# Linear attention: all four banks of masked scores through ScalarE's copy and GpSimd's select, none through VectorE

## The chip, the cores and the metric

One Trainium2 chip, one of its cores. The metric is the time of one execution on the device in microseconds (us), and the median of several runs is compared.

## The reference, cut to what matters

Two transformer layers over x of 8 x 1024 x 256 in float32: a half-weighted feed-forward block, attention, and another feed-forward block in each. The change lies in the attention of the first layer, which is linear attention with 16 heads of 16 columns, worked off in chunks, with a causal mask inside a chunk and a running state S between chunks:

```python
def step(S, chunk):
    q_c, k_c, v_c = chunk
    inter = jnp.einsum('bhde,bthe->bthd', S, q_c)
    scores = jnp.einsum('bthd,bshd->bhts', q_c, k_c)
    scores = jnp.where(causal, scores, 0.0)
    intra = jnp.einsum('bhts,bshd->bthd', scores, v_c)
    S = S + jnp.einsum('bthd,bthe->bhde', v_c, k_c)
    return (S, inter + intra)
```

The second layer's attention is softmax attention with 16 heads over all 1024 positions, causal. The feed-forward blocks of the second layer have a small router and low-rank experts.

## The kernel before, in words

The kernel works on the batch rows one after another. For each of the eight rows there are two "fronts" (c = 0 and c = 1, 512 tokens each), which compute the first layer and the beginning of the second, and two "tails" with the rest of the second layer. Beside them runs the "core", the softmax attention of an earlier row, cut into 768 steps: at each step TensorE computes score tiles (`tscore`, L798), ScalarE turns them into exponentials (`core_act`, L1343), TensorE multiplies these by the values (`values`, L817) at every other step, and a further product (`score`, L783) feeds the row maxima that VectorE takes (L1137, L1140). GpSimd makes the diagonal blocks of the exponentials causal (L1497).

The order is written out by hand. Every stage is a generator for each engine. `weave` runs a common count of ticks: in a tick it issues the core's first part, then the next piece of front 0, the core's second part, the piece of front 1, and so on. `STEPS` says how many core steps (0, 1 or 2) a tick has, and a batch row takes 120 ticks with 96 steps. An engine takes its instructions strictly in the order in which `weave` issued them, so an instruction that waits holds everything issued behind it.

The fronts and tails of all rows share three PSUM banks in turn (`f_take`, `f_filled`, `f_freed`, `f_gone`): the n-th taker may start when the taker of n - 3 has been read out of its bank.

The linear attention of one front (`lin_pe`, `lin_dve`, `lin_act`, `lin_pool`) handles four blocks j of 128 tokens, in three ticks each, here called the first, second and third tick of j. Its scores for 16 heads fill four banks sc0 to sc3:

- first tick: TensorE computes the output of block j - 1 (L648, L655) and then, in `scores(j, 0)`, the banks sc0 and sc1 (L620, eight matmuls);
- second tick: after the core's `tscore`, TensorE computes in `scores(j, 1)` the banks sc2 and sc3 (L620 again), and then `state` (L631). It takes both banks before its first matmul. VectorE masks sc0 and sc1 in `masked` (L944), from PSUM to the SBUF tile `scm`. ScalarE copies out the output of j - 1 (L1249);
- third tick: ScalarE, after the exponentials of that tick's core step and after the piece of front 0 if the block is front 1's, copies sc2 and sc3 to `scm` in `raw` (L1245), and GpSimd zeroes their upper half in place in `select` (L1409). Then `state` on VectorE (L956) and on GpSimd (L1422).

Which bank `scores(j, 1)` has to wait for depends on what other takers lie between. With none, sc2 takes the bank of the block output of j - 1 and sc3 that of sc0. Where another stage's matmul takes a bank between sc1 and sc2 (this is so in blocks 1 and 2 of front 0, and 0 and 1 of front 1), sc2 needs the bank of sc0 and sc3 that of sc1.

Of the kernel before, what the change touches and what calls it, by code (L numbers as in the profile page):

```python
# [12 lines left out]
ALU = mybir.AluOpType  # L13
# [3 lines left out]
P = 128  # L17
# [7 lines left out]
NC = T // CH  # L25
G = 4
# [31 lines left out]
def macaron(nc, a, out):  # L58
    ctx = ExitStack()
    with ctx:  # L60
        def sb(name, shape, dt=F32):
            return ctx.enter_context(nc.sbuf_tensor(name, shape, dt))

        def sem(name):
            return ctx.enter_context(nc.semaphore(name))
# [15 lines left out]
        mask01 = sb("mask01", [P, P])  # L81
# [32 lines left out]
        def ar(at, *shape):  # L114
            n = math.prod(shape)
            at = int(at * KB)
            v = arena[:, at:at + n]
            names = "abcd"[:len(shape)]
            return v.rearrange(f"p ({' '.join(names)}) -> p {' '.join(names)}", **dict(zip(names[1:], shape[1:]))) if len(shape) > 1 else v
# [10 lines left out]
        scm = ar(27, G, CH)  # L130
# [36 lines left out]
        def ps(i, n=1):  # L167
            return bank[i // 2][:, (i % 2) * CH:(i % 2) * CH + n * CH]
# [210 lines left out]
        s = {n: sem(n) for n in plain_names}  # L379
# [76 lines left out]
        if True:  # L456

            with nc.Block() as block:
# [10 lines left out]
                def f_bank(*key):  # L469
                    return ps(5 + ftab[key] % 3)  # L470

                def f_filled(eng, *key):
                    eng.wait_ge(s["f_full"], ftab[key] + 1)

                def f_freed(*key):
                    return f_free[ftab[key] % 3]

                def f_gone(eng, *key):
                    eng.wait_ge(f_free[ftab[key] % 3], ftab[key] // 3 + 1)
# [107 lines left out]
                def lin_pe(c, b):  # L587
# [47 lines left out]
                    def outputs(j):  # L635
                        t = 4 * c + j
                        if t == 1:
                            f_gone(nc.tensor, 0, b, "st", 0)
                        elif t:
                            nc.tensor.wait_ge(s["st"], 6 * b + t - 1)  # L640
                        nc.tensor.wait_ge(s["vs"][c], 4 * b + j + 1)
                        for i in range(2):
                            f_gone(nc.tensor, c, b, "sc", j, i)
                        nc.tensor.wait_ge(s["sel"][c], 8 * b + 2 * j + 2)
                        bk = f_take(c, b, "y", j)
                        if t:
                            for k in range(KT):
                                mm(bk[:, k * P:(k + 1) * P], ssb[:, (t - 1) % 2, k], qT[:, k, j * P:(j + 1) * P], start=k == 0,  # L648
                                   stop=False, skip_group_check=True)
                        vrow = vlin[:, j].rearrange("p q d -> p (q d)")  # L650
                        for k in range(KT):
                            for o in range(2):
                                for r in range(G):
                                    at = 3 * DK * (4 * k + r) + DK * o
                                    last = mm(bk[HP * r:HP * (r + 1), k * P:(k + 1) * P], vrow[:, at:at + HP],  # L655
                                              scm[:, r, (2 * k + o) * P:(2 * k + o + 1) * P], start=t == 0 and k == 0 and o == 0,
                                              stop=o == 1, skip_group_check=True, tile_position=(0, HP * r))
                        last.then_inc(s["f_full"], 1)
# [208 lines left out]
                def updated(q, b, n):  # L867
                    nc.vector.wait_ge(s["xu"][q], 4 * b + n)
# [53 lines left out]
                def lin_dve(c, b):  # L922
                    yield from ln_dve(c, b, 1, xns, lambda: updated(c, b, 2))
                    yield from idle(4)
                    for j in range(4):
                        nc.vector.wait_ge(s["ksq"][c], 4 * b + j + 1)
                        nc.vector.reduce_sum(kvar[:, j], ksq[:, j % 2].rearrange("p (h d) -> p h d", h=H), AX).then_inc(s["kvar"][c], 1)
                        yield
                    nc.vector.wait_ge(s["kvar"][c], 4 * b + 4)
                    kvf, krf, ktf = (v[:].rearrange("p t h -> p (t h)") for v in (kvar, krs, ktmp))  # L930
                    nc.vector.tensor_scalar(kvf, kvf, EPS, None, ALU.add).then_inc(s["newton"][c], 1)
                    nc.vector.wait_ge(s["newton"][c], NEWTON * b + 1)
                    rsqrt(krf, kvf, ktf, s["newton"][c], NEWTON * b + 1)
                    yield

                    def masked(j):
                        if c == 0 and j == 0 and b >= 3:
                            for o in range(NC):
                                nc.vector.wait_ge(s["xout"][o], 16 * (b - 2))
                        elif c == 0 and j == 0 and b:  # L940
                            nc.vector.wait_ge(s["qkout"][1], 64 * b)
                        for i in range(2):
                            f_filled(nc.vector, c, b, "sc", j, i)
                            nc.vector.tensor_tensor(scm[:, i].rearrange("p (j c) -> p j c", j=G),  # L944
                                                    f_bank(c, b, "sc", j, i).rearrange("p (j c) -> p j c", j=G),
                                                    mask01[:].unsqueeze(1).broadcast_to([P, G, P]), ALU.mult).then_inc(
                                                        f_freed(c, b, "sc", j, i), 1)

                    def state(j):
                        t = 4 * c + j  # L950
                        if t == NT - 1:
                            return
                        f_filled(nc.vector, c, b, "st", j)
                        if t >= 2:
                            nc.vector.wait_ge(s["st"], 6 * b + t - 1)
                        nc.vector.tensor_tensor(smask if t else ssb[:, 0],  # L956
                                                f_bank(c, b, "st", j)[:, 0:D].rearrange("p (k c) -> p k c", k=KT),
                                                bdmask[:].rearrange("p h d -> p (h d)").unsqueeze(1).broadcast_to([P, KT, P]),
                                                ALU.mult).then_inc(f_freed(c, b, "st", j), 1)

                    def added(p):
                        f_filled(nc.vector, c, b, "lo", p)
                        xs = xq(c)[:, 2 * p:2 * p + 2]
                        nc.vector.tensor_tensor(xs, xs, f_bank(c, b, "lo", p).rearrange("p (t c) -> p t c", t=2), ALU.add).then_inc(
                            f_freed(c, b, "lo", p), 1)

                    for j in range(4):
                        if j == 3:
                            added(0)
                        yield  # L970
                        masked(j)
                        yield
                        state(j)
                        yield
                    yield from idle(3)
                    added(1)
                    yield
# [231 lines left out]
                def lin_act(c, b):  # L1209
# [27 lines left out]
                    def raw(j):  # L1237
                        if c == 0 and j == 0 and b >= 3:
                            for o in range(NC):
                                nc.scalar.wait_ge(s["xout"][o], 16 * (b - 2))  # L1240
                        elif c == 0 and j == 0 and b:
                            nc.scalar.wait_ge(s["qkout"][1], 64 * b)
                        for i in (2, 3):
                            f_filled(nc.scalar, c, b, "sc", j, i)
                            nc.scalar.copy(scm[:, i], f_bank(c, b, "sc", j, i)).then_inc(f_freed(c, b, "sc", j, i), 1)  # L1245

# [132 lines left out]
                def lin_pool(c, b):  # L1379
# [23 lines left out]
                                                ALU.mult).then_inc(s["vs"][c], 1)  # L1403

                    def select(j):
                        for i in (2, 3):
                            f_gone(nc.gpsimd, c, b, "sc", j, i)
                            v = scm[:, i].rearrange("p (j c) -> p j c", j=G)
                            nc.gpsimd.affine_select(out=v, in_=v, compare_op=ALU.is_ge, fill=0.0, base=0, pattern=[[0, G], [1, P]],  # L1409
                                                    channel_multiplier=-1).then_inc(s["sel"][c], 1)  # L1410
# [236 lines left out]
```

## Time and profile before

| | |
|---|---|
| median of 3 runs | 2860.79 us (2854.37 to 2863.7) |
| the profiled execution | 2854.86 us, of which the span from the first to the last instruction 2853.1 us |
| mean granted TensorE clock | 0.946 of full speed |
| busy share of the span | TensorE 91%, VectorE 65%, ScalarE 43%, GpSimd 26% |
| chain of work that ended last | TensorE 71%, VectorE 16%, ScalarE 2%, GpSimd 1%, DMA 1% |

The busy share is a mean over stages with different limits; the chain follows back from the last instruction to what released each step. Batch rows 2 to 7 of the linear attention repeat nearly the same pattern, about 331 us apart; the rows of the trace are taken from batch row 4 (front 0 at 1300 to 1344 us, front 1 at 1370 to 1416 us).

### The profile page before, as it was taken

To read this page: it belongs to the slowest core of one execution; us is meant where nothing else is said; L and a number is where in the kernel's file an instruction comes from. 1 tells how busy PE (TensorE), PEld (TensorE's weight loads), DVE (VectorE), ACT (ScalarE), POOL (GpSimd) and SP (SyncE) were. 2 spreads that over 40 slices of the span, in tenths; PEclk is the share of its full clock that TensorE was granted. 3 is DMA by queue.
4 is the path that set the end of the run, shared out by engine and by line. 5 is a ranking of instruction groups with operands and counts; after the bars stand their busy time and mean duration, and the time that the engine had idled before them with its cause. 6 is when DMAs were issued, how large, how long until landed. Compare 5 with 4: busy or idle time off the path is not lost.

```text
span 2853.1 us, 45542 instructions
## 1 busy us (share of the span) xinstructions
PE 2595.9 (91%) x15278; PEld 1723.8 (60%) x15278; DVE 1841.9 (65%) x5524; ACT 1228.5 (43%) x2805; POOL 747.9 (26%) x1285
## 2 busy tenths in 40 slices
PE   5875899989999999999999999999999999998996
PEld 4663566556656666566655666566665666655644
DVE  4454666776667667676676766776667766776642
ACT  2321244454444444444444444454444444444452
POOL 2421222223222232223322232222222233221111
PEclk8996899999999999999999999999999999999998
DMA  2024013411334112422145113332134221343311
GB/s 61 1 68 119 18 24 75 128 39 30 72 88 108 41 43 64 130 64 58 24 110 131 37 32 72 94 102 54 29 79 124 55 58 36 103 112 74 80 31 48
DMA packets 135248, 193.93 MB, mean 68 GB/s; under 512 B 46239, under 2 KB 108014, under 8 KB 124654
## 3 DMA queue, kind: packets, MB, share of 16 engines
q1 hardware_dynamic: 133440, 190.89, 26.4%
q8 instruction: 129, 2.11, 0.3%
q14 instruction: 97, 0.79, 0.1%
q10 hardware_dynamic: 1582, 0.13, 0.0%
HBM read 122.29 MB, written 67.63 MB: 67 GB/s over the span
## 4 chain that ended last, share of the span: by engine, by line
PE 71%; DVE 16%; issue 2%; ACT 2%; POOL 1%; DMA 1%; SPq 0%; DVEq 0%; ACTq 0%; POOLq 0%
PE bank L798 10%; PE bank L817 9%; PE bank L783 9%; PE bank L620 4%; PE bank L711 4%; DVE bank L1137 4%; PE bank L551 4%; PE bank L569 4%; PE bank L600 3%; PE bank L560 3%; PE bank L725 3%; PE bank L530 3%; PE bank L712 2%; PE bank L655 2%; PE bank L768 2%
## 5 line engine op out<-in xcount | busy, mean ns | idle before, releaser
L1343 ACT ACTIVATE pexp<-bank 128x512 f32<-128x512 f32 (+3 forms) x1536 | 677.3, 499 | 575.4 <-PE bank L798 575.2
L1137 DVE CUSTOM_DVE_ANT_0 bank<-bank,maskneg 128x256 f32<-128x256 f32 (+3 forms) x1024 | 484.1, 511 | 263.0 <-PE bank L783 258.9
L798 PE MATMUL bank<-stq,stk 128*128 128x512 f32 (+3 forms) x1536 | 547.5, 427 | 30.9 <-ACT pexp L1343 24.1
L783 PE MATMUL bank<-stk,stq 128*128 128x512 f32 (+3 forms) x1536 | 506.4, 394 | 62.5 <-DVE mxa L1137 24.6
L798 PEld LDWEIGHTS bank<-stq,stk 128*128 128x128 f32 x1536 | 267.9, 195 | 320.1 <-ACT pexp L1343 190.5
L1140 DVE TENSOR_REDUCE mxa<-bank 128x1 f32<-128x512 f32 x512 | 345.8, 683 | 146.5 <-PE bank L783 142.3
L1497 POOL TENSOR_SCALAR_AFFINE_SELECT pexp<-pexp 128x256 f32<-128x256 f32 x512 | 212.4, 422 | 763.6 <-ACT pexp L1343 763.4
L783 PEld LDWEIGHTS bank<-stk,stq 128*128 128x128 f32 x1536 | 281.5, 198 | 174.4 <-issue 136.0
L817 PE MATMUL bank<-pexp,vsm 128*32 128x512 f32 (+3 forms) x3072 | 343.8, 521 | 20.1 <-POOL pexp L1497 19.9
L1409 POOL TENSOR_SCALAR_AFFINE_SELECT arena<-arena 128x512 f32<-128x512 f32 x128 | 78.2, 634 | 393.4 <-ACT arena L1245 393.3
L530 PE MATMUL bank<-ident,arena 128*128 128x128 f32 x768 | 117.9, 301 | 46.7 <-DVE arena L861 42.6
L620 PE MATMUL bank<-arena 32*128 32x256 f32 x1024 | 152.3, 416 | 8.6 <-DVE arena L944 5.6
L944 DVE TENSOR_TENSOR arena<-bank,mask 128x512 f32<-128x512 f32 x128 | 82.3, 684 | 92.6 <-PE bank L620 92.6
L530 PEld LDWEIGHTS bank<-ident,arena 128*128 128x128 f32 x768 | 101.5, 157 | 64.9 <-DVE arena L861 46.6
L551 PE MATMUL bank<-arena,wk 128*128 128x256 f32 x512 | 133.1, 410 | 4.7 <-DVE arena L885 4.5
L817 PEld LDWEIGHTS bank<-pexp,vsm 128*32 128x32 f32 x3072 | 62.7, 110 | 123.3 <-issue 94.7
L1162 ACT COPY xnT<-bank 128x512 f32<-128x512 f32 x160 | 88.6, 601 | 96.6 <-PE bank L530 96.0
L1360 POOL TENSOR_SCALAR varep<-mv 128x4 f32<-128x4 f32 x96 | 22.5, 234 | 408.6 <-DVE mv L855 408.2
L620 PEld LDWEIGHTS bank<-arena 32*128 32x128 f32 x1024 | 92.1, 193 | 56.3 <-issue 37.9
L861 DVE TENSOR_SCALAR arena<-x,mv,rstd 128x256 f32<-128x256 f32 x320 | 117.9, 429 | 11.4 <-POOL rstd L1362 10.7
L560 PE MATMUL bank<-wr,arena 128*128 128x256 f32 x512 | 122.9, 383 | 0.1
L551 PEld LDWEIGHTS bank<-arena,wk 128*128 128x128 f32 x512 | 104.7, 208 | 27.6 <-issue 6.1
(186 smaller groups left out, 4051.6 us busy)
## 6 DMA issues: line engine op xcount, KB each, us to landing
stq<-q_halves SPq DMA_DIRECT2D x128, 256.0 KB
arena<-rope_table SPq DMA_DIRECT2D x16, 1024.0 KB
q_halves<-arena SPq DMA_DIRECT2D x32, 512.0 KB, 2.8
k_halves<-arena SPq DMA_DIRECT2D x32, 512.0 KB, 2.9
stk<-k_halves SPq DMA_DIRECT2D x64, 256.0 KB
stk<-k_halves SPq DMA_DIRECT2D x128, 128.0 KB
v_rows<-arena SPq DMA_DIRECT2D x16, 544.0 KB, 4.1
vsm<-v_rows SPq DMA_DIRECT2D x16, 544.0 KB, 3.8
```

What stands on the lines that cost most here:

```text
L530: last = nc.tensor.transpose(bk[:, t * P:(t + 1) * P], src[:, t, k * P:(k + 1) * P], ident[:])
L551: last = mm(bk[:, m * D:(m + 1) * D], wk0[:, k, m * P:(m + 1) * P], xmA[:, h, k], start=k == 0, stop=k == KT - 1)
L560: last = mm(bk[:, i * D:(i + 1) * D], xmB[:, p, k, i * P:(i + 1) * P], wr0[:, k], start=k == 0, stop=k == KT - 1)
L620: last = mm(bks[i][:, k * D:(k + 1) * D], khT[rows, k, j * P:(j + 1) * P], qbd[rows, j % 2, k], start=k == 0, stop=k == KT - 1, skip_group ...
L783: last = mm(bk[:, col:col + n], stq[b_][:, h % 2, qb * P:(qb + 1) * P], stk[b_][:, h % 2, k0:k0 + n], start=True, stop=True)
L798: mm(ps(j)[:, 0:n], stk[b_][:, j, kb * P:(kb + 1) * P], stq[b_][:, j, (c + 1) * CH - n:(c + 1) * CH], start=True, stop=True).then_inc(s["t ...
L817: last = mm(ps(2)[HP * j:HP * (j + 1), CH - n:CH], vsm[:, kb, at:at + HP], pexp[:, (u - 1 + j // 2) % NPX, j % 2, 0:n], start=kb == 0, sto ...
L861: nc.vector.tensor_scalar(dst[:, t], xs[:, t], mv[:, q, t, 0:1], rstd[:, q, t:t + 1], ALU.subtract, ALU.mult).then_inc(s["xn"][q], 1)
L1137: last = nc.vector.tensor_tensor_reduce(out=sc, in0=sc, in1=maskneg[:, CH - n:CH], scale=1.0, scalar=LOWEST, op0=ALU.add, op1=ALU.max, acc ...
L1140: last = nc.vector.reduce_max(dst, sc, AX)
L1343: nc.scalar.activation(pexp[:, u % NPX, j, 0:n], ps(j)[:, 0:n], ACT.Exp, scale=DK ** -0.5).then_inc(s["exp_done"], 1)
L1497: nc.gpsimd.affine_select(out=v, in_=v, compare_op=ALU.is_ge, fill=0.0, base=0, pattern=[[0, 2], [1, P]], channel_multiplier=-1).then_inc( ...
```

## The change

`masked` on VectorE goes, with its 128 tensor_tensor instructions. ScalarE's `raw` copies all four banks in the third tick, and GpSimd's `select` works on all four. The count of GpSimd's selects for which TensorE's output waits doubles accordingly.

```diff
                         for i in range(2):
                             f_gone(nc.tensor, c, b, "sc", j, i)
-                        nc.tensor.wait_ge(s["sel"][c], 8 * b + 2 * j + 2)
+                        nc.tensor.wait_ge(s["sel"][c], 16 * b + 4 * j + 4)
...
-                    def masked(j):
-                        if c == 0 and j == 0 and b >= 3:
-                            for o in range(NC):
-                                nc.vector.wait_ge(s["xout"][o], 16 * (b - 2))
-                        elif c == 0 and j == 0 and b:
-                            nc.vector.wait_ge(s["qkout"][1], 64 * b)
-                        for i in range(2):
-                            f_filled(nc.vector, c, b, "sc", j, i)
-                            nc.vector.tensor_tensor(scm[:, i].rearrange("p (j c) -> p j c", j=G),
-                                                    f_bank(c, b, "sc", j, i).rearrange("p (j c) -> p j c", j=G),
-                                                    mask01[:].unsqueeze(1).broadcast_to([P, G, P]), ALU.mult).then_inc(
-                                                        f_freed(c, b, "sc", j, i), 1)
-
...
-                        masked(j)
...
-                        for i in (2, 3):
+                        for i in range(0, 4):
                             f_filled(nc.scalar, c, b, "sc", j, i)
                             nc.scalar.copy(scm[:, i], f_bank(c, b, "sc", j, i)).then_inc(f_freed(c, b, "sc", j, i), 1)
...
                     def select(j):
-                        for i in (2, 3):
+                        for i in range(0, 4):
                             f_gone(nc.gpsimd, c, b, "sc", j, i)
```

## Rows read from the trace of the kernel before

**Rows 1.** The page's first part: busy time, share of the span, instructions.
```profile
PE 2595.9 (91%) x15278; PEld 1723.8 (60%) x15278; DVE 1841.9 (65%) x5524; ACT 1228.5 (43%) x2805; POOL 747.9 (26%) x1285
```

**Rows 2.** Windows of both fronts' linear attention: busy us (instructions), PEclk, DMA, GB/s.
```profile
1300.00:1344.00 44.00, 44.00 (x380) 32.14 (x380) 28.48 (x75) 20.15 (x46) 14.78 (x30) 1.00 0.22 52
1370.00:1416.00 46.00, 45.73 (x331) 31.45 (x331) 28.12 (x67) 18.21 (x37) 14.08 (x24) 0.93 0.13 27
```

**Rows 3.** Groups by line: mask, copy and select.
```profile
L1409 POOL TENSOR_SCALAR_AFFINE_SELECT arena<-arena 128x512 f32<-128x512 f32 x128 | 78.2, 634 | 393.4 <-ACT arena L1245 393.3
L944 DVE TENSOR_TENSOR arena<-bank,mask 128x512 f32<-128x512 f32 x128 | 82.3, 684 | 92.6 <-PE bank L620 92.6
L1245 ACT COPY arena<-bank 128x512 f32<-128x512 f32 x128 | 68.8, 589 | 87.0 <-PE bank L620 87.0
```

**Rows 4.** Timeline, front 0, block 1: start, us, instruction.
```profile
1312.32 1.13 PE L620 MATMUL bank<-arena 32*128 32x256 f32 x8
...
1316.76 1.13 PE L620 MATMUL bank<-arena 32*128 32x256 f32 x8
...
1316.90 0.66 ACT L1343 ACTIVATE pexp<-bank 128x256 f32<-128x256 f32 x2
...
1317.93 1.07 ACT L1245 COPY arena<-bank 128x512 f32<-128x512 f32 x2 [0.37 <-PE bank L620]
...
1318.58 1.22 POOL L1409 TENSOR_SCALAR_AFFINE_SELECT arena<-arena 128x512 f32<-128x512 f32 x2 [5.45 <-ACT arena L1245]
```

**Rows 5.** Timeline, front 0, blocks 0, 2 and 3: last ScalarE work, second half.
```profile
1303.01 1.09 ACT L1343 ACTIVATE pexp<-bank 128x512 f32<-128x512 f32 x2 [1.37 <-PE bank L798]
...
1305.08 1.13 PE L620 MATMUL bank<-arena 32*128 32x256 f32 x8
...
1329.43 1.13 PE L620 MATMUL bank<-arena 32*128 32x256 f32 x8
...
1329.48 0.45 ACT L1343 ACTIVATE pexp<-bank 128x128 f32<-128x128 f32 x2 [2.94 <-PE bank L798]
...
1337.67 1.09 ACT L1343 ACTIVATE pexp<-bank 128x512 f32<-128x512 f32 x2 [1.15 <-PE bank L798]
...
1338.03 1.13 PE L620 MATMUL bank<-arena 32*128 32x256 f32 x8
```

**Rows 6.** Timeline, front 1, blocks 0, 2 and 3: the same, and a mask.
```profile
1378.46 0.60 ACT L1183 ACTIVATE arena<-bank 128x512 f32<-128x512 f32 x1 [2.48 <-PE bank L551]
1378.59 0.73 PEld L620 LDWEIGHTS bank<-arena 32*128 32x128 f32 x8 [0.35 <-issue]
...
1402.66 1.08 ACT L1343 ACTIVATE pexp<-bank 128x512 f32<-128x512 f32 x2 [1.15 <-PE bank L798]
...
1404.38 0.73 PEld L620 LDWEIGHTS bank<-arena 32*128 32x128 f32 x8 [0.24 <-issue]
...
1411.31 1.29 DVE L944 TENSOR_TENSOR arena<-bank,mask 128x512 f32<-128x512 f32 x2 [0.29 <-PE bank L620]
1411.75 0.87 ACT L1343 ACTIVATE pexp<-bank 128x384 f32<-128x384 f32 x2 [1.09 <-PE bank L798]
...
1412.75 0.73 PEld L620 LDWEIGHTS bank<-arena 32*128 32x128 f32 x8 [0.84 <-DVE arena L944]
```

**Rows 7.** Windows over two idle gaps of TensorE and what follows each.
```profile
1511.30:1513.10 1.80, 0.02 (x1) 0.06 (x1) 1.76 (x9) 0.74 (x2) 0.65 (x2) 1.00 0.82 291
...
1514.20:1517.60 3.40, 3.40 (x16) 2.68 (x13) 2.80 (x10) 0.90 (x3) 0.67 (x2) 0.50 0.01 2
...
1553.00:1554.20 1.20, 0.04 (x1) 0.00 (x0) 1.20 (x9) 0.12 (x1) 0.70 (x2) 1.00 1.12 353
1554.20:1557.00 2.80, 2.77 (x23) 1.96 (x24) 2.02 (x9) 1.64 (x4) 1.22 (x3) 1.00 0.67 213
```

**Rows 8.** Windows of the same work in batch rows 4 and 5.
```profile
1302.25:1374.07 71.82, 69.94 (x496) 45.93 (x494) 47.62 (x131) 33.34 (x81) 24.51 (x44) 0.98 0.14 34
1636.22:1706.52 70.30, 68.42 (x495) 45.42 (x494) 46.10 (x129) 33.34 (x81) 24.52 (x44) 1.00 0.15 35
```

## The prediction

> **What bounds the kernel now.** I read the page first: TensorE is busy for 2595.9 of 2853.1 us, VectorE for 1841.9, ScalarE for 1228.5, GpSimd for 747.9 [rows 1]. That alone says that work taken from VectorE need not show and that work given to ScalarE need not hurt. What counts is the stretch in which the change lies, so I read the windows of the linear attention next. Front 0 takes 44 us there and TensorE is busy for all 44.00; front 1 takes 46 us and it is busy for 45.73, while VectorE works for 28.48 and 28.12, and ScalarE for 20.15 and 18.21 [rows 2]. In these stretches TensorE is the bound, and the chain of work that ended last runs through TensorE from block to block. So the question is one of order: does TensorE ever have to wait for a read-out that VectorE used to do early and ScalarE now does late? For that I read the groups of the three operations [rows 3] and then, block by block, the timeline [rows 4 to 6].
>
> **What the change removes and adds.** Removed from VectorE: 128 masks of 684 ns, 82.3 us busy in the trace [rows 3]. They lie beside a TensorE that is never idle, so I price the removal at nothing. Added to ScalarE: 128 copies of 589 ns, 75 us; added to GpSimd: 128 selects of 634 ns, 81 us [rows 3]. Both engines wait most of that time anyway: in block 1 of front 0 ScalarE waited 0.37 us for sc2 before its copies, and GpSimd 5.45 us before its selects [rows 4]. The first two selects of a block can run while TensorE fills sc2 and sc3, and the last select still ends about one select after the last copy. So the output's wait for GpSimd is late only by what TensorE itself is late. These instructions cost nothing as work.
>
> **What the change moves.** The reading of sc0 and sc1 moves from the second tick on VectorE to the third tick on ScalarE, behind that tick's exponentials. But `scores(j, 1)`, in TensorE's second tick, needs the bank of sc0 and in four of eight blocks that of sc1 too. Behind its wait in TensorE's queue stand sc2 and sc3, `state`, the core's values and scores and the next `tscore`, for which ScalarE, VectorE and GpSimd wait in turn. There is no deadlock in that: the exponentials ahead of ScalarE's copies need only the `tscore` issued just before.
>
> The new stall of a block is the time at which ScalarE has emptied the needed bank, less the time at which TensorE started the second half before. Three constants come from rows: two copies take 1.07 us together [rows 4] at 0.59 each [rows 3], so the second starts 0.48 after the first; an instruction that waits for nothing starts the same 0.11 before the reported end of the one ahead (0.59 less 0.48). So after the end of ScalarE's previous instruction sc0 is free at +0.48 and sc1 at +0.96. And TensorE starts 0.15 after the release: masks until 1412.60, matmuls from 1412.75 [rows 6]. A stall is therefore the ScalarE end + 0.63 (sc0 needed) or + 1.11 (sc1 needed), less the old start.
>
> Front 0:
> - Block 0 (sc0): its third tick has no core step. ScalarE is free at 1304.10, + 0.63 = 1304.73, before the old start at 1305.08 [rows 5]: 0.
> - Block 1 (sc1): 1317.56 + 1.11 - 1316.76 = 1.91 us [rows 4].
> - Block 2 (sc1): 1329.93 + 1.11 - 1329.43 = 1.61 us [rows 5].
> - Block 3 (sc0): 1338.76 + 0.63 - 1338.03 = 1.36 us [rows 5].
>
> Front 1:
> - Block 0 (sc1): 1379.06 + 1.11 - 1378.59 = 1.58 us; block 1 repeats the same pattern, with the receptance's tanh in place of the relu: 1.58 us [rows 6].
> - Block 2 (sc0): 1403.74 + 0.63 = 1404.37, just in time for 1404.38 [rows 6]: 0.
> - Block 3 (sc0): 1412.62 + 0.63 - 1412.75 = 0.50 us [rows 6]. Here TensorE had waited for the mask already, and that wait is in the old start.
>
> That is 8.54 us for a batch row. Since TensorE has no slack in these stretches, it is late by this afterwards, and the chain is with it. `state` needs sc1's bank where sc3 needs only sc0's; sc1 is out 0.48 us after sc0 while the second half takes 1.13 us [rows 5], so no second wait follows. Batch rows 2 to 7 have this pattern: 6 x 8.54 = 51 us. For rows 0 and 1, with no or little core work and so with ScalarE sooner at hand, I bound each by nothing and 8.5 us and take 10 us for both. Direct stalls: 61 us (51 to 68).
>
> **The clock.** Five stalls of a batch row last 1.36 to 1.91 us, in a TensorE that had none there. What an idle gap does is seen elsewhere: after a gap of 1.8 us at 1511 us the granted clock was 0.50 (1.2 in place of 2.4 GHz) for 3.4 us, after one of 1.2 us at 1553 us it stayed at 1.00 [rows 7]. The new stalls lie between these two, nearer to the longer one. The price of a fall is bounded above by 3.4 x 0.5 = 1.7 us, where TensorE would have been busy throughout. The same work took 71.82 us in batch row 4 at a mean clock of 0.98 and 70.30 in row 5 at 1.00 [rows 8]: 1.5 us. I take 1.5, and three of the five stalls with a fall (bounds none and five): 4.5 us a row, 27 for six rows, 3 for the first two: 30 us (0 to 60).
>
> The Trainium skill, "TensorE: Matmul & The Clock Gate" (HAM oscillation), warns of waits for data longer than any stall worked out here; if only those count, no fall comes and the sum stays at 61 us. Rows 7 speak against it, since a gap of 1.8 us was followed by a lower clock.
>
> The last row of rows 6 also shows TensorE's queue at such a wait: 0.84 us idle for the mask, with nothing taken ahead. The same page (Architectural detail) says that weight loads can be pulled ahead of matmuls in flight; eight such loads take 0.73 us in rows 6, 0.09 each, and if one were ahead at each of five stalls in six rows, the stalls would come to 58 in place of 61 us.
>
> **The sum.** 61 + 30 = 91 us. Against the profiled execution (2854.9 us: its span of 2853.1 and 1.8 around it) that is 2946 us. The runs' median lies 5.9 us above that execution, so I forecast 2952 us, 3.2% slower.
>
> **Rivals.**
> - Stalls without falls of the clock: 2861 + 61 = 2922 us. For it: the stalls are shorter than the gap that brought a fall in rows 7. Chance 0.22.
> - Half of the delay is won back later, because VectorE, ScalarE and the transfers run ahead while TensorE stands, and TensorE's later waits for them shrink: 2861 + 30 = 2891 us. For it: outside these stretches TensorE is not always busy (91% over the span). Against: most of these waits follow a serial chain that starts from TensorE's own result and is shifted with it. Chance 0.10.
> - Every one of the five stalls brings a fall, or falls that last longer, and the first two batch rows stall fully: 68 + 60 = 128 and more, 2989 us and up. Chance 0.08.
> - Faster: VectorE sets the pace (it has 16% of the chain that ended last), and the 82.3 us taken from it come off the end: at most 2861 - 82 = 2779 us. It decides if TensorE's waits for the masks and for the maxima queued behind them are worth more than 8.5 us a batch row. Against: one wait for a mask of 0.84 us stands in rows 6, and rows 2 leave 0.27 us of idle time in 90. Chance 0.05.
> - No change: TensorE's wait is hidden after all, because ScalarE reaches its copies before TensorE the second half in nearly all blocks, as in blocks 0 and 2 of the two fronts. 2861 us. It would need ScalarE 1.4 to 1.9 us earlier. Chance 0.05.
> - My forecast, with one to four falls in a batch row: 0.50. Its own range is 2932 to 2972 us.
>
> **Range and chances.** From the rival without falls, a little widened towards the one that wins some back, up to all five falls: 2900 to 2990 us. A measurement of this kernel can tell about 0.3% from no change, 8.6 us. Slower 0.90, same 0.05, faster 0.05.
>
> **What the next profile would show.** If right: TensorE's L620 waits for ScalarE's L1245 in blocks 1, 2, 3 of front 0 and 0, 1, 3 of front 1, by 1.3 to 2 us (0.5 in the last), about 50 us in all; block 0 of front 0 and block 2 of front 1 without a wait. TensorE's busy share in the two windows falls from all to about nine tenths, the distance between batch rows grows from 331 to 340 us or more, and new stretches at clock 0.50 stand behind the stalls. L1245 and L1409 count 256 each at unchanged durations. The prediction is wrong if L620 does not wait, if the distance of the batch rows grows by much less than the stalls' sum (then it is won back), or if TensorE's later waits for VectorE shrink by as much.

## The result, and the profile after

The changed kernel takes 2945.23 us (median of 4 runs, 2925.3 to 2951.69) against 2857.58 us (4 runs); the ratio is 1.0294, 95% interval 1.0268 to 1.0320. It is slower by some 85 us. The forecast was 2952 us, 3.2% slower. The profiled execution took 2942.78 us, its span is 2941.0 us.

The first part of the page of the changed kernel, which answers to [rows 1], and from its fifth part the groups that answer to [rows 3] (lines below 944 have moved up by 13 or 14, so the copy is L1231, the select L1395, the exponentials L1329):

```profile
PE 2618.4 (89%) x15278; PEld 1751.6 (60%) x15278; DVE 1769.8 (60%) x5396; ACT 1292.4 (44%) x2933; POOL 833.7 (28%) x1413
...
L1395 POOL TENSOR_SCALAR_AFFINE_SELECT arena<-arena 128x512 f32<-128x512 f32 x256 | 160.8, 653 | 382.6 <-ACT arena L1231 382.6
L620 PE MATMUL bank<-arena 32*128 32x256 f32 x1024 | 151.6, 413 | 66.0 <-ACT arena L1231 63.0
L1231 ACT COPY arena<-bank 128x512 f32<-128x512 f32 x256 | 137.8, 595 | 84.1 <-PE bank L620 84.1
```

VectorE gave up 72 us of busy time, ScalarE and GpSimd took over 64 and 86, and none of this is the loss (the first experiment keeps all of it and loses nothing). The loss is in TensorE's row: before `scores` (L620) it now sits idle for 66.0 us, 63.0 of it until ScalarE's copy; in the kernel before it was 8.6 us. TensorE's idle time over the span rose from 257.2 (2853.1 less 2595.9 [rows 1]) to 322.6 us (2941.0 less 2618.4), by 65.4 us. Its busy time rose by 22.5 us, though it does the same 15278 matmuls: some of them ran at the lower clock. The two make the 87.9 us by which the span grew.

The windows of the linear attention in batch row 4, which answer to [rows 2]:

```profile
1337.00:1382.00 45.00, 40.33 (x309) 29.27 (x308) 21.96 (x60) 19.42 (x44) 17.38 (x31) 0.96 0.17 38
1414.00:1460.00 46.00, 42.56 (x325) 30.35 (x318) 21.58 (x56) 20.64 (x41) 17.02 (x29) 0.96 0.13 27
```

A TensorE that was busy for 44.00 of 44 us is now busy for 40.33 of 45. The timeline of front 0, block 1 shows why ([rows 4] before), and under it stand the second halves of front 0, blocks 2 and 3, and of front 1, blocks 0, 1 and 3 ([rows 5, 6] before):

```profile
1352.63 0.59 PE L798 MATMUL bank<-stq,stk 128*128 128x256 f32 x2
...
1353.51 0.66 ACT L1329 ACTIVATE pexp<-bank 128x256 f32<-128x256 f32 x2
1354.04 1.09 ACT L1231 COPY arena<-bank 128x512 f32<-128x512 f32 x2
...
1355.25 0.76 PEld L620 LDWEIGHTS bank<-arena 32*128 32x128 f32 x8 [2.12 <-ACT arena L1231]
1355.28 1.13 PE L620 MATMUL bank<-arena 32*128 32x256 f32 x8 [1.84 <-ACT arena L1231]
...
1371.11 1.13 PE L620 MATMUL bank<-arena 32*128 32x256 f32 x8 [1.54 <-ACT arena L1231]
...
1381.07 1.13 PE L620 MATMUL bank<-arena 32*128 32x256 f32 x8 [1.28 <-ACT arena L1231]
...
1419.95 1.13 PE L620 MATMUL bank<-arena 32*128 32x256 f32 x8 [1.51 <-ACT arena L1231]
...
1436.08 1.13 PE L620 MATMUL bank<-arena 32*128 32x256 f32 x8 [1.51 <-ACT arena L1231]
...
1457.81 1.13 PE L620 MATMUL bank<-arena 32*128 32x256 f32 x8 [0.42 <-ACT arena L1231]
```

TensorE computes the score tiles of the core, then wants the banks of sc0 and sc1. ScalarE first makes the exponentials of just these tiles (1353.51 to 1354.17), then copies sc0 and sc1 (until 1355.13), and TensorE goes on 0.15 us later.

### The profile page after: what moved, and what is told of

Read it like the earlier page. It is cut to its first block, busy times and chain, and to the rows that moved or that the text cites. A ratio compares the mean times of both kernels' runs of the same rounds, so it can differ in the third digit from the quotient of the medians.

```text
span 2941.0 us, 45663 instructions
## 1 busy us (share of the span) xinstructions
PE 2618.4 (89%) x15278; PEld 1751.6 (60%) x15278; DVE 1769.8 (60%) x5396; ACT 1292.4 (44%) x2933; POOL 833.7 (28%) x1413
## 4 chain that ended last, share of the span: by engine, by line
PE 69%; DVE 14%; ACT 4%; issue 3%; DMA 2%; POOL 1%; SPq 1%; DVEq 0%; ACTq 0%; POOLq 0%
PE bank L798 9%; PE bank L783 8%; PE bank L817 8%; PE bank L620 4%; PE bank L711 4%; PE bank L551 4%; DVE bank L1123 3%; PE bank L569 3%; PE bank L560 3%; PE bank L600 3%; PE bank L725 3%; PE bank L530 3%; PE bank L712 2%; PE bank L655 2%; PE bank L768 2%
## 5 line engine op out<-in xcount | busy, mean ns | idle before, releaser
L1329 ACT ACTIVATE pexp<-bank 128x512 f32<-128x512 f32 (+3 forms) x1536 | 677.1, 498 | 573.9 <-PE bank L798 573.5
L817 PE MATMUL bank<-pexp,vsm 128*32 128x512 f32 (+3 forms) x3072 | 336.7, 511 | 20.2 <-POOL pexp L1483 20.0
L1395 POOL TENSOR_SCALAR_AFFINE_SELECT arena<-arena 128x512 f32<-128x512 f32 x256 | 160.8, 653 | 382.6 <-ACT arena L1231 382.6
L620 PE MATMUL bank<-arena 32*128 32x256 f32 x1024 | 151.6, 413 | 66.0 <-ACT arena L1231 63.0
L1231 ACT COPY arena<-bank 128x512 f32<-128x512 f32 x256 | 137.8, 595 | 84.1 <-PE bank L620 84.1
L620 PEld LDWEIGHTS bank<-arena 32*128 32x128 f32 x1024 | 94.7, 190 | 112.1 <-ACT arena L1231 66.5
L1346 POOL TENSOR_SCALAR varep<-mv 128x4 f32<-128x4 f32 x96 | 22.6, 235 | 409.8 <-DVE mv L855 409.4
L560 PE MATMUL bank<-wr,arena 128*128 128x256 f32 x512 | 130.1, 400 | 0.1
```

The source lines that it names most:

```text
L560: last = mm(bk[:, i * D:(i + 1) * D], xmB[:, p, k, i * P:(i + 1) * P], wr0[:, k], start=k == 0, stop=k == KT - 1)
L620: last = mm(bks[i][:, k * D:(k + 1) * D], khT[rows, k, j * P:(j + 1) * P], qbd[rows, j % 2, k], start=k == 0, stop=k == KT - 1, skip_group ...
L817: last = mm(ps(2)[HP * j:HP * (j + 1), CH - n:CH], vsm[:, kb, at:at + HP], pexp[:, (u - 1 + j // 2) % NPX, j % 2, 0:n], start=kb == 0, sto ...
L1329: nc.scalar.activation(pexp[:, u % NPX, j, 0:n], ps(j)[:, 0:n], ACT.Exp, scale=DK ** -0.5).then_inc(s["exp_done"], 1)
```

## The experiments

All ratios are against the kernel before on the same chip. In the diffs the comments behind # are added here, and where a run changes how many banks ScalarE and GpSimd take, the counts that TensorE waits for change with it. After each expectation stands what was measured; the profiled executions of all of them are put together behind the last one.

**ScalarE early.** The changed kernel, with the copies of sc0 and sc1 one tick earlier on the same engine.

```diff
-                    def raw(j):
+                    def raw(j, part):
...
-                        for i in range(0, 4):
+                        for i in (2 * part, 2 * part + 1):
...
                         if j:
                             heads_out(j - 1)
+                        raw(j, 0)
                         yield
-                        raw(j)
+                        raw(j, 1)
```

> The changed kernel, but ScalarE copies sc0 and sc1 in the second tick (right after the output of j - 1) and sc2 and sc3 in the third. The work on every engine is that of the changed kernel. If the loss is the order (ScalarE reads sc0 and sc1 only after the third tick's exponentials), it is gone: sc0 and sc1 are free before TensorE wants their banks, and the time is that of the kernel before, 2850 to 2868 us. If the loss is the added work of ScalarE (64 us more busy) and GpSimd (86 us more busy), it stays: 2935 to 2955 us.

Measured: 2859.9 us (10 runs) against 2856.25, ratio 1.0003, interval 0.9986 to 1.0020. The whole loss is gone, with every operation of the change still in place. The group of TensorE's `scores` and that of the copies in this run:

```profile
L620 PE MATMUL bank<-arena 32*128 32x256 f32 x1024 | 152.1, 416 | 6.0 <-ACT arena L1231 3.0 <-POOL arena L1381 2.2 <-ACT arena L1220 0.9
L1231 ACT COPY arena<-bank 128x512 f32<-128x512 f32 x256 | 137.6, 590 | 112.2 <-PE bank L620 112.2
```

The same 256 copies, but it is now ScalarE that waits for TensorE. Its timeline in front 0, block 1:

```profile
1308.85 1.13 PE L620 MATMUL bank<-arena 32*128 32x256 f32 x8
...
1310.01 1.07 ACT L1231 COPY arena<-bank 128x512 f32<-128x512 f32 x2 [0.56 <-PE bank L620]
...
1313.29 1.13 PE L620 MATMUL bank<-arena 32*128 32x256 f32 x8
```

ScalarE empties sc0 and sc1 by 1311.08, and TensorE needs them at 1313.29.

**VectorE late.** The kernel before, with the masks one tick later on VectorE.

```diff
-                        masked(j)
                         yield
+                        masked(j)
                         state(j)
```

> The kernel before, but VectorE's masks moved to the third tick, ahead of its state. No engine gets any work that it had not. If lateness alone costs, TensorE's second half waits for VectorE, which first takes the maxima of the tick before: in block 1 of front 0 its masks would end at about 1318.8 where the second half started at 1316.76, a stall of about 2.2 us, and now in block 0 too. 2940 to 3020 us. If the added work on ScalarE and GpSimd is the cause, nothing changes: 2850 to 2870 us.

Measured: 3062.68 us (4 runs), ratio 1.0724, interval 1.0682 to 1.0766. No engine has more to do than in the kernel before, and it is the slowest of all. The theory of the order holds in kind, but the time is a miss: it lies 43 us above the upper end of my range. Front 0, block 1:

```profile
1408.88 0.70 DVE L1137 CUSTOM_DVE_ANT_0 bank<-bank,maskneg 128x512 f32<-128x512 f32 x1 [4.59 <-PE bank L783]
...
1409.49 1.28 DVE L944 TENSOR_TENSOR arena<-bank,mask 128x512 f32<-128x512 f32 x2
1410.89 1.30 PEld L620 LDWEIGHTS bank<-arena 32*128 32x128 f32 x8 [2.38 <-DVE arena L944]
1410.92 2.00 PE L620 MATMUL bank<-arena 32*128 32x256 f32 x8 [2.08 <-DVE arena L944]
```

And a window of this run that begins just behind that stall:

```profile
1411.00:1417.80 6.80, 6.80 (x24) 5.18 (x24) 1.30 (x5) 1.07 (x2) 3.35 (x6) 0.50 0.00 0
```

The stall of 2.08 us is the one foretold (2.2). The matmuls behind it took 2.00 us for what takes 1.13 elsewhere [rows 4], with the granted clock at 0.50.

**GpSimd's half.** The kernel before, with VectorE copying in place of masking, and GpSimd selecting all four banks.

```diff
-                            nc.vector.tensor_tensor(scm[:, i]..., f_bank(c, b, "sc", j, i)..., mask01..., ALU.mult)
+                            nc.vector.tensor_copy(scm[:, i], f_bank(c, b, "sc", j, i))
...
-                        for i in (2, 3):      # select on GpSimd
+                        for i in range(4):
```

> The kernel before, but VectorE copies sc0 and sc1 unmasked, in the second tick as before, and GpSimd selects all four banks. That is GpSimd's part of the change alone: 128 more selects, and the output waits for them. By my theory it costs nothing, 2850 to 2868 us, since the first two selects run before the third copy ends. If the selects are what is late, 2 more of 0.63 us in each of 64 blocks, up to 80 us more: 2900 to 2940 us.

Measured: 2864.09 us (10 runs) against 2856.25, ratio 1.0023, interval 1.0007 to 1.0038. The 128 selects more cost some 7 us at the most (2 to 11 by the interval) of the 85. In the profile the idle time is the same as before (257.3 us for 257.2) and TensorE's busy time is 6 us longer at a clock of 0.944 for 0.946, so the few us lie in the clock; that the selects bring this about is not shown, since the run with ScalarE early has as many selects and a ratio of 1.0003. TensorE's wait for them before the output was 2.9 us in this run, in 9 waits, so it is no new wait: that of the changed kernel is 2.9 us in 9 too, and the kernel before had 3.1 in 9.

**One bank late.** Only sc0 goes to ScalarE's third tick; sc1 stays with VectorE's mask.

```diff
-                        for i in range(2):    # masked on VectorE
+                        for i in (1,):
...
-                        for i in (2, 3):      # raw on ScalarE, select on GpSimd
+                        for i in (0, 2, 3):
```

> Only sc0 moves to ScalarE's third tick, sc1 stays with VectorE's mask in the second. By the theory of the order the four stalls that ended with sc1 end with sc0, 0.48 us earlier, the others stay: 8.3 less 1.9 is 6.4 us a batch row, with some fewer falls of the clock: 2912 to 2935 us. If the loss went with the number of banks that ScalarE and GpSimd take over, half of it would stay: 2900 us. If only stalls long enough for a fall of the clock counted, most would be gone: below 2890 us.

Measured: 2952.09 us (4 runs), ratio 1.0323, interval 1.0282 to 1.0364: a miss, no faster than with both banks late. The stalls did shrink, the four that had ended with sc1, by 0.35 to 0.42 us each where I had worked out 0.48: TensorE's wait for ScalarE's copies is 50.1 us in place of 63.0. Its whole idle time is 22.6 us less than in the changed kernel, about 10 us more than these stalls account for. But its busy time is 27.9 us more, because the mean granted clock fell from 0.942 to 0.931. Windows over three stalls of this run, each followed by one of what came after, and the beginning of front 1:

```profile
1351.71:1353.17 1.46, 0.00 (x0) 0.00 (x1) 0.76 (x2) 1.20 (x4) 0.19 (x1) 1.00 0.00 0
1355.20:1358.60 3.40, 3.40 (x11) 2.46 (x10) 1.01 (x5) 0.21 (x1) 3.14 (x6) 0.50 0.00 0
1367.57:1368.71 1.14, 0.01 (x1) 0.00 (x1) 1.10 (x2) 0.92 (x3) 0.16 (x1) 1.00 0.04 14
1369.00:1373.00 4.00, 4.00 (x29) 2.88 (x27) 2.42 (x10) 2.16 (x4) 2.55 (x5) 1.00 1.05 229
1377.41:1378.66 1.25, 0.00 (x0) 0.00 (x1) 1.25 (x7) 1.14 (x3) 0.05 (x1) 1.00 0.00 0
1379.10:1385.90 6.80, 6.80 (x35) 5.43 (x32) 2.13 (x9) 3.18 (x7) 2.83 (x6) 0.50 0.28 82
...
1413.20:1423.40 10.20, 9.71 (x30) 5.53 (x29) 6.34 (x10) 2.13 (x5) 2.91 (x4) 0.50 0.00 0
```

A stall of 1.25 us was followed by 6.8 us at the lower clock with TensorE busy throughout, some 3.4 us of loss; and where front 1 begins, the clock stayed low for 10.2 us. That place is not without a fall in the kernel before either:

```profile
1370.80:1377.60 6.80, 6.80 (x25) 4.05 (x18) 5.45 (x9) 1.09 (x2) 1.52 (x2) 0.50 0.00 0
```

**The other bank late.** The same work moved, but sc1 in place of sc0.

```diff
-                        for i in (1,):        # masked on VectorE
+                        for i in (0,):
...
-                        for i in (0, 2, 3):   # raw on ScalarE, select on GpSimd
+                        for i in (1, 2, 3):
```

> As the run with one bank late, but the other bank: sc0 stays with VectorE's mask in the second tick, sc1 moves to ScalarE's third. The same work moves between the engines. By the theory of the order only the four blocks whose second half needs sc1 stall, by ScalarE's end + 0.63 less the old start: 1.43, 1.13, 1.10 and 1.10, and block 3 of front 0 by some 0.3 at its state: 5.1 us a batch row, 35 to 40 us, and 0 to 40 us from stretches of the lower clock, which the run with sc0 late showed to be larger than I had taken: 2895 to 2935 us. If work moved is what costs, it is the 2952 us of that run.

Measured: 2909.09 us (4 runs), ratio 1.0168, interval 1.0150 to 1.0185, within the range of the order and 43 us below the run with the other bank late. TensorE's idle time is 35 us above that of the kernel before, as worked out. So the time does not go with how much work has moved: the same work costs 50 us here and 96 there. Of the difference between the two profiled executions the order accounts for 8 us, the idle time; 30 us are TensorE's longer busy time, at a clock of 0.931 for 0.939.

**sc0 copied twice.** The changed kernel, with one more copy on ScalarE ahead of the release of sc0.

```diff
                             f_filled(nc.scalar, c, b, "sc", j, i)
+                            if i == 0:
+                                nc.scalar.copy(scm[:, 3], f_bank(c, b, "sc", j, i))
```

> The changed kernel with one copy more on ScalarE in each block, of sc0 and ahead of its release. Each stall becomes 0.48 us longer and block 2 of front 1 gets one of about 0.45: 7 x 0.48 is 3.4 us a batch row, 24 us over seven, and some more stretches of the lower clock, up to 10 us: 2965 to 2985 us. If ScalarE's copies cost only as work hidden beside TensorE, the 64 more of them (31 us busy) change nothing against the changed kernel: 2945 us.

Measured: 3004.52 us (4 runs), ratio 1.0493, interval 1.0463 to 1.0523. Slower, as the order says, but by 59 us more than the changed kernel where I expected 20 to 40. In its profile the idle time rose by 26 us, as worked out (24). The profiled execution is the slowest of the four (3025.49 us, clock 0.921; the others 0.927 to 0.931), and in it TensorE's busy time is 57 us longer than in the changed kernel; at the median that leaves about 33 us to the clock, where I had taken up to 10.

**Roles swapped.** ScalarE copies sc0 and sc1 in the second tick with GpSimd's select; VectorE masks sc2 and sc3 in the third.

```diff
-                        for i in range(2):    # masked on VectorE, now in the third tick
+                        for i in (2, 3):
...
-                        for i in (2, 3):      # raw on ScalarE, now in the second tick; select on GpSimd
+                        for i in range(2):
```

> ScalarE copies sc0 and sc1 in the second tick and GpSimd selects them; VectorE masks sc2 and sc3 in the third tick, which need no select behind them. By the theory of the order there is no stall at the second half; the end of a block is a mask (0.68 us) in place of a copy and a select. If VectorE is at hand in the third tick, the waits of the output for GpSimd (3 us in all before) go: 2840 to 2860 us. If VectorE comes late to sc2, the next taker of its bank waits: 2865 to 2900 us.

Measured: 2864.75 us (10 runs) against 2860.53, ratio 1.0015, interval 1.0003 to 1.0027. No gain: a tie with the kernel before, and the time lies between the two ranges. TensorE's wait for GpSimd before the output is gone, as expected, but the idle time over the span is 6 us more. No version here beats the kernel before.

**The changed kernel again.**

> The changed kernel unchanged, for the spread of its times and clocks. If the part of its loss beyond the stalls is lost to stretches of lower clock, the time of a run goes with its mean granted clock, and a run at the clock of the kernel before (0.946) takes its time plus the idle time added alone, 2855 + 65 = 2920 us, where 0.938 gives some 2950 us. If the clock were beside the point, runs at equal clock would differ as much as runs at different ones.

Measured: 2938.96 us (6 runs), ratio 1.0278, interval 1.0253 to 1.0303. The six runs with their mean clocks: 2925.49 (0.946), 2932.61 (0.944), 2937.96 (0.942), 2939.96 (0.942), 2950.33 (0.938), 2950.67 (0.939). Time times clock is 2767 to 2771 us in all six, while the times spread over 25 us: the spread is the clock's. The fastest run, at the clock of the kernel before, lies 5 us above the 2920 us expected.

The profiled executions side by side (idle is the span less TensorE's busy time; the last two columns are the differences from the kernel before, us):

| | span | TensorE busy | idle | clock | idle more | busy more |
|---|---|---|---|---|---|---|
| before | 2853.1 | 2595.9 | 257.2 | 0.946 | | |
| changed | 2941.0 | 2618.4 | 322.6 | 0.942 | 65 | 22 |
| changed, again | 2936.2 | 2615.2 | 321.0 | 0.942 | 64 | 19 |
| ScalarE early | 2852.9 | 2595.4 | 257.5 | 0.946 | 0 | 0 |
| GpSimd's half | 2859.3 | 2602.0 | 257.3 | 0.944 | 0 | 6 |
| roles swapped | 2861.1 | 2597.6 | 263.5 | 0.947 | 6 | 2 |
| sc1 late | 2908.1 | 2616.1 | 292.0 | 0.939 | 35 | 20 |
| sc0 late | 2946.3 | 2646.3 | 300.0 | 0.931 | 43 | 50 |
| sc0 twice | 3023.8 | 2675.6 | 348.2 | 0.921 | 91 | 80 |
| VectorE late | 3053.3 | 2682.2 | 371.1 | 0.921 | 114 | 86 |

## Why the prediction was right, step by step

**The bound.** Right. TensorE had no slack in these stretches, and what it waited there was added to the end. Nothing of it was won back later: the idle time over the whole span grew by 65 us, no less than the 61 us priced for the stalls, and TensorE's waits for VectorE are 158 us in all for 160 before. The other signs came too: the first `scores` of batch rows 3 to 7 lie 340 to 342 us apart (328 to 334 before), and TensorE is busy for 90% and 93% of the two windows.

**Work removed and added at no cost.** Right, and shown: with all the copies and selects in place and only their tick changed, the ratio is 1.0003; GpSimd's half alone is 1.0023. The mean copy and select took a little longer, 595 and 653 ns for 589 and 634.

**The stalls.** Right to 0.02 us each. In batch row 4 the second half began 1.84 us after the end of TensorE's last matmul in block 1 of front 0 (worked out 1.91 between old and new start), 1.54 in block 2 (1.61), 1.28 in block 3 (1.36), 1.51 in blocks 0 and 1 of front 1 (1.58 each), 0.42 in its block 3 (0.50); the two blocks that were to have no stall have none. These rows count 0.07 us less than the distance from start to start, since matmuls without a wait between them overlap by so much (in the same timeline L620 ends at 1356.41 and L631 starts at 1356.34). The direct stalls were priced at 61 us; TensorE's idle time before `scores` grew by 57 us (66.0 less 8.6) and by 8 us at other lines, 65 in all. Of the 63.0 us of waits for ScalarE's copies, batch rows 2 to 7 have 48.6 (worked out 51) and rows 0 and 1 have 14.4; there 5.0 us of waits for VectorE's masks went in return, so that these two rows gave 9.4 of the 10 us that I had taken between bounds. One reading was wrong without an effect on this sum: the 0.84 us in the last row of [rows 6] is the idle time of the weight loads, while TensorE's matmuls ran on until 1412.82, as this line of the kernel before shows, and so had no gap before 1412.75. That no weight load of `scores` is taken ahead of the wait holds in the changed kernel as well: the loads start at 1355.25, 0.03 us before their matmuls. The line of the kernel before:

```profile
1411.76 1.06 PE L817 MATMUL bank<-pexp,vsm 128*32 128x512 f32 x8
```

**The clock.** Here the size was off, at 30 us for 22. I had five stalls in a batch row of which three bring a fall. (I called them shorter than the gap of 1.8 us in [rows 7]; the longest, worked out at 1.91 and measured at 1.84, is not.) Windows over stalls of the changed kernel, and behind each what followed:

```profile
1353.44:1355.25 1.81, 0.00 (x1) 0.00 (x1) 0.76 (x2) 1.70 (x5) 0.54 (x1) 1.00 0.00 0
1356.90:1360.30 3.40, 3.40 (x11) 2.80 (x10) 1.30 (x5) 0.59 (x2) 3.23 (x6) 0.50 0.00 0
1369.57:1371.08 1.51, 0.00 (x0) 0.00 (x0) 1.31 (x2) 1.40 (x4) 0.54 (x1) 1.00 0.22 49
1371.50:1375.00 3.50, 3.50 (x27) 2.42 (x24) 2.04 (x10) 2.09 (x4) 2.42 (x4) 1.00 1.07 229
...
1418.44:1419.92 1.48, 0.00 (x1) 0.00 (x0) 0.76 (x2) 1.37 (x3) 0.53 (x1) 1.00 0.00 0
1421.70:1425.10 3.40, 3.40 (x13) 2.94 (x12) 1.98 (x7) 0.46 (x1) 3.00 (x5) 0.50 0.23 51
1434.57:1436.05 1.48, 0.00 (x1) 0.00 (x0) 0.87 (x4) 1.37 (x3) 0.53 (x1) 1.00 0.00 0
1437.00:1441.00 4.00, 4.00 (x25) 2.60 (x23) 1.72 (x3) 2.06 (x4) 3.00 (x5) 1.00 0.00 0
```

Two of the five brought a fall in this batch row, and of two stalls of the same 1.48 us one did and one did not. Counted in the same way over batch rows 2 to 7, 14 of the 30 stalls of over 1 us were accompanied or followed within 3 us by a lower clock, and 15 of 30 in the second trace of the changed kernel, where I had taken 18: that is the part of the term that shows as too large. The bound from above for the price of a fall, 1.7 us, is the one that fits where TensorE is busy throughout. The Trainium skill, "TensorE: Matmul & The Clock Gate" (HAM oscillation), warns in that section only of longer waits; here the trace decides against the reading that only those count, with falls behind 1.81 and 1.48 us, and behind 1.25 in the run with sc0 late. The same page of the Trainium skill has a formula for the penalty (Terms: the time at the lower level times what the level lacks). An estimate by it comes near the 22 us: by the mean clocks the lower level held for 2 x 0.058 x 2941 = 341 us against 2 x 0.054 x 2853 = 308 before, and half of the 33 us more is 17.

**The sum.** 61 + 30 = 91 us, measured 65 + 22 = 88 in the profile. The terms were off by 4 and 8 us in opposite ways, so part of the closeness of the sum is luck. The step from the profiled execution to the median of the runs was off too: I added 5.9 us, and it is 2.5 (2945.23 less 2942.78).

**The rivals.** Stalls without falls: the fastest runs of the changed kernel, 2925 us, come within 4 us of it, the others do not. Half won back and no change are refuted by the idle time, which grew by more than the stalls. Faster is refuted by the run with ScalarE early: there VectorE is rid of its 128 masks, TensorE waits 3.0 us in all for ScalarE's copies before `scores`, and the ratio is 1.0003. All five falls did not come in the changed kernel, but did next to it: with sc0 copied twice 29 of 30 stalls came with a lower clock. And sc0 late has shorter stalls and 50 us of clock: had the change been built so, my range would have held the time and my working would not have given it.

**What stays open.** Why the lower clock takes 50 us with sc0 late and 20 to 22 with sc1 late or both late. The four runs of sc0 late all lie at 0.924 to 0.933, the ten of the changed kernel at 0.938 to 0.947, so it is no chance of one run. The stalls themselves are not the answer: in the traces the lower level held for 407 us with sc0 late and for 342 in the changed kernel, and of these 65 us only about 5 lie in the linear attention of batch rows 2 to 7; some 50 lie in the stages between, in the same rows, and the rest before and after. Why the clock falls more often there, where no operation was moved, no run here shows. In those stages traces of equal times differ as well: 86 us at the lower level in the kernel before, 70 and 94 in two runs within 0.3% of it.

## What to carry to other kernels

An operation handed to an engine with time to spare also takes a new place in that engine's order, and it is the place that is to be priced: find who waits for the bank that it releases, read when the new engine gets there in the old trace, and take the difference to the start of the waiting instruction. That needs two rows and a release time for each case, and here it gave every stall to less than a tenth of a us. If the receiving engine can be reached one step earlier in its queue, the transfer is free, but where TensorE is the bound it then brings nothing either.

## What the runs showed of the hardware beyond the prediction

Idle gaps of TensorE of some 0.4 to 2.7 us cost through the clock between a third of the gaps themselves and a little more than they: 65 us of idle time came with 22 us of slower matmuls, 35 with 20, 91 with 80, 114 with 86, 43 with 50.

How often the granted clock was below full speed between the beginning of a gap and 3 us behind its end goes with the length of the gap. Counted over the gaps of more than 1 us before `scores`, in batch rows 2 to 7 of the six traces that have such gaps (changed twice, VectorE late, sc0 late, sc1 late, sc0 twice):

| gap, us | gaps | with a lower clock |
|---|---|---|
| 1.02 to 1.17 | 34 | 0 |
| 1.28 to 1.55 | 66 | 31 |
| 1.60 to 1.91 | 31 | 27 |
| 1.95 to 2.70 | 53 | 50 |

So a stall that is made longer can cost more than its own length: with sc0 copied twice each stall grew by about half a us, and those with a lower clock rose from 14 to 29 of 30. In the same places the kernel before has no gap of over 1 us, and from 2 us before the first to 2 us behind the start of the last `scores` of each front the lower level held for 24 us in these six batch rows, for 66 in the changed kernel.

In the changed kernel time times mean granted clock is constant within 7 us (2767 to 2774) over ten runs whose times differ by 26. The same product follows the idle time from kernel to kernel. Its median is 2703 us over 19 runs of the kernel before (2699 to 2714). ScalarE early and GpSimd's half lie within 1 us of that, and above it lie roles swapped by 4 us (idle time more: 6), sc1 late by 33 (35), sc0 late by 35 (43), the changed kernel by 66 (65), sc0 twice by 85 (91) and VectorE late by 111 (114). For these kernels the product is the steadier measure of what the order costs, the clock left out.
